# Attention over 40 fields: the shift by the maxima as four matmuls on quarters of the array

## The reference

```python
q = (einsum('bfe,oe->bfo', x, Wq) + bq).reshape(B, F, 4, 32)      # k and v likewise
att = softmax(einsum('bfhd,bghd->bhfg', q, k) / 8, axis=-1)
out = einsum('bhfg,bghd->bfhd', att, v).reshape(B, F, 128)
y = relu(out + einsum('bfe,oe->bfo', x, Wr) + br)
```

## Time and profile before

| | us |
|---|---|
| median of 3 runs | 1023.21 (1017.99 to 1023.76) |
| the profiled execution, its own time | 1000.4 |
| its span, first to last instruction | 998.6 |
| granted TensorE clock, mean | 0.995 of 2.4 GHz |
| PE busy, share of the span | 950.5 (95%) |
| PEld busy | 716.4 (72%) |
| DVE busy | 725.8 (73%) |
| ACT busy | 769.0 (77%) |
| POOL busy | 878.2 (88%) |
| L401 (the shift), PE busy, 512 matmuls | 114.3 |

### The profile page before, as it was taken

How to read it: one execution, slowest core, us unless ns; L and a number is a source line. 1 busy time by engine, 2 the same in 40 slices (tenths; PEclk the granted TensorE clock), 3 DMA queues, 4 the chain that set the end, 5 groups by cost and what they waited for, 6 DMA issues and landing times.

```text
span 998.6 us, 69163 instructions
## 1 busy us (share of the span) xinstructions
PE 950.5 (95%) x30464; PEld 716.4 (72%) x30464; DVE 725.8 (73%) x2065; ACT 769.0 (77%) x1541; POOL 878.2 (88%) x1028
## 2 busy tenths in 40 slices
PE   5999999999998999999999999999999999999996
PEld 3777777777776777777777777766777777777774
DVE  4777777777776777777777777767777777777775
ACT  3778878877777778778777777867787787887886
POOL 2989989988988989999889888988998999998996
PEclk9999999999999999999999999999999999999998
DMA  4333433333333334334334333433334443343321
GB/s 128 100 111 124 120 112 115 121 118 107 114 117 107 121 110 124 119 113 123 113 117 124 107 122 109 124 98 116 111 120 124 110 121 111 121 124 112 119 86 66
DMA packets 63338, 113.80 MB, mean 114 GB/s; under 512 B 9536, under 2 KB 9792, under 8 KB 63040
## 3 DMA queue, kind: packets, MB, share of 16 engines
q1 hardware_dynamic: 63040, 109.37, 36.2%
HBM read 67.39 MB, written 41.94 MB: 109 GB/s over the span
## 4 chain that ended last, share of the span: by engine, by line
PE 95%; issue 3%; ACT 1%; DMA 0%; DVE 0%; POOL 0%; SPq 0%; POOLq 0%; ACTq 0%
PE vr_bank L389 24%; PE o_bank L422 21%; PE s_buf L376 18%; PE o_bank L361 10%; PE s_buf L401 10%; PE o_bank L360 7%; PE vr_bank L394 4%; PE vr_bank L392 1%; DMA vr_bias<-vr_bias_in 0%; ACT rv L236 0%; ACT y_rows L216 0%; POOL y_sum L173 0%; POOL m_diag L165 0%; POOLq L33 0%; ACT q_flat L209 0%
## 5 line engine op out<-in xcount | busy, mean ns | idle before, releaser
L173 POOL TENSOR_TENSOR y_sum<-rv,y_att 128x512 f32<-128x512 f32 x256 | 302.3, 1181 | 64.7 <-ACT y_rows L216 60.2
L165 POOL TENSOR_TENSOR m_diag<-m_split,ident 128x640 bf16<-128x640 bf16 x256 | 322.3, 1259 | 32.9 <-DVE m_split L314 29.4
L389 PE MATMUL vr_bank<-w_cols,xT 64*128 64x128 f32 x2048 | 298.3, 286 | 3.7 <-issue 2.6
L389 PEld LDWEIGHTS vr_bank<-w_cols,xT 64*128 64x128 f32 x2048 | 248.4, 188 | 72.1 <-ACT rv L236 38.3
L181 POOL TENSOR_SCALAR q_bd<-q_flat,consts 128x320 f32<-128x320 f32 x512 | 265.9, 532 | 19.2 <-ACT q_flat L209 19.2
L209 ACT ACTIVATE q_flat<-o_bank,biases 128x320 f32<-128x320 f32 x256 | 134.9, 527 | 183.4 <-PE o_bank L361 183.4
L394 PEld LDWEIGHTS vr_bank<-w_cols,xT 64*128 64x128 f32 x2048 | 270.8, 190 | 0.6 <-issue 0.6
L394 PE MATMUL vr_bank<-w_cols,xT 64*128 64x128 f32 x2048 | 270.6, 272 | 0.2 <-issue 0.2
L303 DVE TRANSPOSE_TENSOR_REDUCE s_buf<-s_buf 128x20 f32<-128x640 f32 x256 | 221.5, 865 | 57.7 <-PE s_buf L376 57.7
L236 ACT ACTIVATE rv<-vr_bank 128x1024 f32<-128x1024 f32 x256 | 260.2, 1016 | 0.3 <-POOL y_sum L173 0.3
L298 DVE TENSOR_SCALAR kT<-o_bank,biases 128x320 f32<-128x320 f32 x256 | 141.0, 551 | 150.5 <-PE o_bank L361 150.5
(11 more groups left out here) (30 smaller groups left out, 552.2 us busy)
## 6 DMA issues: line engine op xcount, KB each, us to landing
xT<-xT_in SPq DMA_DIRECT2D x256, 256.0 KB, 2.8
y<-y_rows SPq DMA_DIRECT2D x512, 80.0 KB
w_cols<-w_in SPq DMA_DIRECT2D x1, 128.0 KB, 2.1
vr_bias<-vr_bias_in SPq DMA_DIRECT2D x1, 128.0 KB, 4.9
consts<-consts_in SPq DMA_DIRECT2D x1, 20.0 KB, 2.5
biases<-bias_in SPq DMA_DIRECT2D x1, 1.0 KB, 1.9
```

Of the source, the lines that this page charges most:

```text
L165: pool.tensor_tensor(m_diag[:], m_split[:, place % 2].unsqueeze(2).to_broadcast([P, BLOCKS, QUAD]), ident[:].unsqueeze(1).to_broadcast([P, ...
L173: pool.tensor_tensor(y_sum[:, place % 2].rearrange("r (a d) -> r a d", d=DIM), rv[:, place % 4, 1, :, 0:DIM], y_att[:, place % 2].rearrang ...
L389: nc.tensor.matmul(vr_bank[:, 0, OUT * pair:OUT * (pair + 1)], xT[0:HALF, place % 8, cols], w_cols[0:HALF, 1], start=True, stop=True, skip ...
```

## The change

The two matmuls of shift, one for each bank t of s_buf, over all 128 rows and all 128 columns of the array (2 x 64 columns of pick), become four: for each bank one on rows 0 to 63 and the column half 0, writing 40 partitions from 0 (member 0), and one on rows 64 to 127 and the column half 64, writing 40 partitions from 64 (member 1). Each has 40 weight columns and the same 320 moving columns, bf16. The two of a bank follow each other. The semaphore is set by the last of the four. The rows 40 to 63 of each half of s_buf are no longer written by it. A step then has 121 matmuls and as many weight loads.

```diff
             def shift(n, place):
                 pe.wait_ge(diag_ready, n + 1)
                 for t in range(2):
-                    mm = nc.tensor.matmul(s_buf[place % 2][:, t, 0:TOK], pick[:].rearrange("k m f -> k (m f)"),
-                                          m_diag[:, t * (BLOCKS // 2):(t + 1) * (BLOCKS // 2)].rearrange("k b i -> k (b i)"),
-                                          start=False, stop=True, skip_group_check=True)
+                    for member in range(MEMBERS):
+                        rows = slice(HALF * member, HALF * (member + 1))
+                        mm = nc.tensor.matmul(s_buf[place % 2][HALF * member:HALF * member + FIELDS, t, 0:TOK],
+                                              pick[rows, member, 0:FIELDS],
+                                              m_diag[rows, t * (BLOCKS // 2):(t + 1) * (BLOCKS // 2)].rearrange("k b i -> k (b i)"),
+                                              start=False, stop=True, skip_group_check=True)
                 mm.then_inc(shifted, 1)
```

## The result

The changed kernel took 1037.22 us (median of 20 runs, 1025.43 to 1049.29), the kernel before 1022.83 (20 runs, 1002.64 to 1030.88). The ratio is 1.0237, with a 95% interval of 1.0181 to 1.0294: slower by 2.4%, where 1.0% faster was forecast. The ratio and its interval leave out every run more than 1.5% above the fastest of its kernel (16 of the 20 before, 5 of the 20 changed), while the two medians are of all runs, and their ratio is 1.0141. Slower it is by either, and the time lies above the range.

A forecast was written before the change was run, and what follows sets the result against it. PE bounds the kernel, by its own 3.62 us step or, in about 4 packets of 10, late program delivery. Gain 26 us less 16 given back, net 10: 1012 us from 1023, range 996 to 1028.

The forecast's parts named there:

- Entry: From attend's last matmul start to the first shift start: 0.13 us falls to 0.03, a gain of 0.10 a step.
- the four matmuls: Shift: 0.15 us from first to last start, no change, with 0.01 between a bank's members and 0.14 between banks.
- exit: From the last shift matmul to the values: stays at 0.23 us, bounds 0.10 less and 0 more.
- quiet step: Shift-to-shift time on PE in a step without packet stalls: 3.62 us falls to 3.52, 26 us over 256 steps.
- Who keeps up: Other engines' waits each have 0.10 us less room; none takes the gain; POOL's 3.42 us is the next bound.
- The rival of the members in turn: Shift: a bank's second member waits until the first has streamed, 0.19 us more a step, 1060 us; chance 0.09.
- The delivery of program: PE's instruction packets arrive too late for the shorter, longer-coded step: 16 us given back, bounds 0 and 26 and a little more.
- the 94 late packets: Some 94 stalls at PE's packet ends among 242 packets, each expected to grow by 0.13 us, 12 us together.
- all of it is given back: Late packets eat the 26 us and 4 more add at most 16, or entry gains nothing: 1020 to 1030; chance 0.26.
- slower: Forecast chance that the changed kernel is slower, beyond about 1% (10 us) that can't be told from no change: 0.11.
- the one on the profiled run: Sign of failure: the profiled run and the timed ones differ in their stalls by another amount than now.
- The net: Whole kernel: 26 us gained less 16 given back, 10 us or 1.0%, taken off the median as 1023 - 11 = 1012.

The follow-up runs named there:

- whole_four: Kernel before with each bank's shift matmul over the whole array cut into two of 160 columns, 246 instructions a step: 1038.1 us, ratio 1.0123.

## Why the prediction was wrong

- *Entry, the four matmuls, exit:* right. 0.03, 0.15 and 0.23 were forecast, -0.01, 0.16 and 0.23 measured; the quiet step fell by 0.12 to 0.13 where 0.10 was said. That is 31 us over all steps where 26 were said, and with the packets mostly out of the way 22.5 us of them arrived.
- *Who keeps up:* right. Nothing in the changed kernel's quiet step waits longer.
- *The rival of the members in turn:* did not occur. The two members of a bank start 0.03 apart and stream together. The Trainium skill, "TensorEngine Tiling (Array Packing)", Gotcha 1, has row tiles barred from one PSUM bank at the same time; in this trace two row tiles that write different partitions of one bank did not wait for each other.
- *The delivery of program:* this term failed. It was seen, named and set at 16 us given back, with "26 us and a little more" as its far bound. Measured, the 31 us of the quiet step and 14 us more were lost at the medians, 45 us in all; between the profiled executions the stalls grew by 63 us. I had sized the term by making the 94 late packets later, 12 us, and had put 3 us on packets that become late and 1 us on the four more packets. The first is the one that hardly happened: a stall on PE measures 0.60 us where it was 0.54. The other two are what came. The stalls on PE went from 47 to 121 in number. And four more packets, where packets are what is late, cost up to their whole 4 us each: the bare count costs 1.2% (whole_four), 12 us, where I had put 1.
- That a late packet takes longer than another is not what the traces show, since stalls that follow each other were 4.9 us apart in the kernel before and are 4.4 apart now. What they show is that the next packet's DMA starts later after an end is passed, 1.56 us in place of 1.35, while its transfer hardly changes, 1.11 us and 1.07.
- The rival "all of it is given back" had the mechanism and a chance of 0.26, but I ended it at 1030 although its own text adds 16 us for the four packets to the 26 eaten. Its far end, 1023 + 16 = 1039, is near the median that came, 1037. By the ratio, 2.4%, the loss is 24 us and beyond it. That the number fits is in part luck, since it puts 16 us on the count, where whole_four measured 12. The chances followed the wrong term: slower had 0.11.
- Of the signs of failure, the one on the profiled run came too: it is 5 us under the median of the timed runs now, where it was 22.
- The net was written once as 10 us and taken off as 11, which changes nothing here.

So the loss comes apart only in part. The bare count costs some 1.2% (1.0123; 1.0070 for half as many). The 31 us of the shorter quiet step, 3% of the time, were given back whole in each of three pairs with equal counts. Two of these pairs are level: changed and whole_four (1.0141 and 1.0143 by the medians of all runs, 1.0237 and 1.0123 with intervals that overlap), and the two with 256 instructions a step (1.0217 and 1.0240). In the third, with 244 instructions, the shorter quiet step, or the tile form that comes with it, lost 1.3% beyond that (0.9993 less 0.9860). Whether the changed kernel lost anything beyond its count and the quiet step is therefore open; and so is why the next packet's DMA starts later after an end when PE has less slack or a wait stands alone. A sequencer that stands at a wait asks for its next packet later would fit it, and fits that moving one wait gained 2.1% at the same quiet step; it was not shown, since the trace has the start of a packet's DMA and not when it is asked for.

## What to carry to other kernels

When a step written out 256 times has hundreds of small matmuls, count its instructions as a resource: here a packet of 256 of TensorE's instructions took 3.87 to 4.1 us on average in the kernels with 240 to 256 instructions a step, and a saving of 31 us on the engine was worth 22.5 us at 198 instructions a step and nothing or less at 244 to 256. Gaps that end with "issue", spaced by 256 instructions, are the sign; what helped here was fewer instructions, fewer waits that need one of their own, and less DMA traffic, and not faster matmuls. If a trace shows that an engine's program is late even part of the time, price an edit by its instructions first, and expect more packets to be late rather than the late ones to be later.

## What the hardware showed that I had not expected

- Where in the step a packet ends changes the time by 4.8% at the same work and count: 0.9975 in attend, 1.0217 at the values, 1.0453 in the scores (the last in another job; within one job it is 2.4%).
- One semaphore wait that stands alone ahead of queries and keys cost 2.1%, though PE's quiet step is 3.62 us with and without it.
- The output's stores, which nothing on PE waits for, cost 4.3% (3.1% by the medians of all runs). The transfer of an instruction packet is 1.11 us with them and 1.09 without, so the cost lies ahead of the transfer.
- The DMA of an instruction packet starts only after TensorE has passed the end before it: one packet in 240 of 241 such intervals in the kernel before, 1.35 us after the end on average, and in 244 of 245 in the changed one, 1.56 us after it.
- The Trainium skill, "Runtime: NRT & Kernel Launch", Instruction fetch mechanics, holds the fetch at block ends to be mostly hidden. In the kernel before the stalls at packet ends took 5% of the span (47 of 998.6 us) and in the changed one 11% (110 of 1030.1).
